# Filling the q and k stacks by 36 transfers inside SBUF instead of a DRAM round trip

## The chip, the cores and the metric

The kernel runs on one core of one Trainium2 chip. The core has five instruction streams that run side by side and meet only at semaphores: PE (TensorE, matrix products), DVE (VectorE), ACT (ScalarE), POOL (GpSimd) and SP (SyncE, which here does nothing but start DMAs). The metric is the device time of one execution in microseconds. Lower is better.

## The reference

The reference is one transformer block. Its first half is a layer norm and a causal linear attention with 16 heads of 16 numbers each; its second half is a layer norm and a mixture of eight experts of which each token uses two.

```python
q = elu(x @ Wq + bq) + 1;  k = elu(x @ Wk + bk) + 1;  v = x @ Wv + bv
s, z = s + outer(k_i, v_i), z + k_i            # over 2048 positions
value_i = (q_i @ s) / (q_i . z + 1e-6)
x = x + values @ Wo + bo
x = x + moe(layernorm(x))                      # top 2 of 8 experts, gelu
```

The input is 4 sequences of 2048 tokens with 256 features, in float32.

## The kernel before

**Stages.** The attention works in 16 steps of 128 positions of all four sequences (512 tokens a step). The recurrence is replaced, within a step, by a masked product of scores and, between steps, by a carried state. The program text is written as a pipeline over steps: body `c` does the front of step `c` (normalise, project q, k and v), the scores and values of step `c-1` and the router of step `c-2`. Every engine has its own copy of `body`, and the order of the work is that of the code on each engine; nothing is scheduled by a planner. Bodies 0 and 1 (the front of the first two steps) are shorter than the others, and body 1 is run in two halves: first its front alone, then its back. After the 16 steps come the tables of the router and then the expert phase, some 71 tiles, which uses none of what is changed.

**Stacks.** PE multiplies in float16. To keep precision, q and k are each split in a high and a low part (`qkhl`, written by ACT at L905 for the high part and by POOL at L1567, or DVE at L1265 in the first two steps, for the low part). A score product has a contraction of only 16 numbers a head, so the kernel stacks three products (high q with high k, low q with high k, high q with low k) for two heads over each other: 96 rows. `kst` and `qst` hold these stacks. Each has two buffers, used in turn by even and odd steps. A row of `qkhl` is a feature on one of 128 partitions, a row of a stack is the same feature on another partition, so the data must cross partitions, and a DMA does that.

**The fill before.** SP writes q's four parts to DRAM (L391, 512 KB), waits for the landing, and reads them back with six loads (L414, 128 KB each). Then it does the same for k, with three loads (L409, 256 KB each). In the first two steps both writes go out first. What frees `qkhl` for the next step is the landing of the write to DRAM (`q_out`, `k_out`, waited for by ACT in `qk_high`). PE waits for all nine loads ahead of the first scores of a step (L559 to L562).

**What else is in SP's queue.** SP runs its DMAs in the order of the code. In a body it is: the load of `xs` for the next step (L375), the store of an output (L378), the load of `xr` (L382), the fill, and then the load of a chunk of the expert weights into `w1raw` (L418 in body 1, L422 otherwise). ACT converts each chunk (`w1_high`, L931). In the second half of body 1 ACT does that between two scores:

```python
                if bk:
                    out_hi(s, 0)
                    score_hi(1, 2)
                    score_hi(1, 3)
                if ro:
                    row_copy(0)
                if c == 1 and not front:
                    w1_high()
```

The landing of the chunk thus stands ahead of ACT's part of the score `(2, 0)` (L875). DVE's `attention_weight` (L1406) gives `wsplit_lo`, which guards the first fill, because the raw weights lie in `kst` at first.

Of the kernel before, what the change touches and what calls it, by code (L numbers as in the profile page):

```python
# [23 lines left out]
P = 128  # L24
B, S, D = 4, 2048, 256
H, HD = 16, 16
E, F = 8, 512
T = B * S
C = 128
# [29 lines left out]
C_TOKEN, C_END = C_PAD + PADS, C_PAD + PADS + STEPS * B  # L59
H_TRI, H_ONES, H_END = 0, 128, 256  # L60
# [27 lines left out]
def build(nc, x, wqkvo, bqk, bv, bo, rw, w1, b1, w2, b2, cf, ch, cb, out):  # L88
    qk_dram = nc.dram_tensor("qk_parts", (2, 2, 4, P, B * C), F16, kind="Internal").ap()
# [4 lines left out]
    with ExitStack() as ctx:  # L94
        def sem(name):
            return ctx.enter_context(nc.semaphore(name))
# [141 lines left out]
        xn_done, xr_in, xr_done = sem("xn_done"), sem("xr_in"), sem("xr_done")  # L238
        xT_ps, xT_hi, xT_lo = sem("xT_ps"), sem("xT_hi"), sem("xT_lo")
        qk_ps, qk_neg, qk_lin, qk_f = sem("qk_ps"), sem("qk_neg"), sem("qk_lin"), sem("qk_f")  # L240
        qk_hi, qk_lo, q_out, k_out = sem("qk_hi"), sem("qk_lo"), sem("q_out"), sem("k_out")
        stack_in = [sem("stack_in0"), sem("stack_in1")]
# [113 lines left out]
        def _(sp):  # L356
# [10 lines left out]
            def body(j, c, front=True, back=True):  # L367
# [3 lines left out]
                lead = fr and c < 2  # L371
# [7 lines left out]
                if fr:  # L379
                    par = c % 2  # L380

                    sp.dma_start(xr[:, par], x_steps[bass.ds(i, 1)].rearrange("i p b d -> p (i b) d")).then_inc(xr_in, 16)  # L382

                    rows = qk_dram[par].rearrange("t (h k) p n -> t h (k p) n", h=2)
                    def send(t, sent):
                        sp.wait_ge(qk_hi, 4 * i + 2 * t + 2)
                        sp.wait_ge(qk_lo, 4 * i + 2 * t + 2)
                        if c >= 2 and t == 0:

                            sp.wait_ge(stack_in[par], 144 * (j + c // 2))  # L390
                        sp.dma_start(qk_dram[par, t].rearrange("m p n -> p m n"), qkhl[:, t]).then_inc(sent, 16)  # L391

                    if lead:
                        send(0, q_out)
                        send(1, k_out)
                    for t, sent in enumerate((q_out, k_out)):
                        if not lead:
                            send(t, sent)
                        sp.wait_ge(sent, 16 * i + 16)
                        if t == 0 and c >= 2:  # L400

                            sp.wait_ge(sc_ps, 16 * (i - 1))
                        elif t == 0:
                            sp.wait_ge(wsplit_lo, 4)
                            sp.wait_ge(qst_zero, 2)
                        for part in range(3):
                            if t == 1:
                                src = rows[1, part // 2].rearrange("(a r) n -> r a n", r=2 * HD)
                                sp.dma_start(kst[2 * HD * part:2 * HD * (part + 1), par], src).then_inc(stack_in[par], 16)  # L409
                                continue  # L410
                            src = rows[0, part % 2].rearrange("(a e d) n -> e d a n", e=2, d=HD)
                            for e in range(2):
                                r0 = 2 * HD * part + HD * e
                                sp.dma_start(qst[r0:r0 + HD, par, :, e], src[e]).then_inc(stack_in[par], 16)  # L414
# [66 lines left out]
        def _(pe):  # L481
# [9 lines left out]
            def body(j, c, front=True, back=True):  # L491
# [67 lines left out]
                def scores(b, n):  # L559
                    g = 16 * s + 4 * b + n  # L560
                    if b == n == 0:
                        pe.wait_ge(stack_in[sp_], 144 * (j + (c - 1) // 2 + 1))  # L562
                    if not fr and b == 0 and n >= 2:

                        pe.wait_ge(v_done, min(2 * (c + 1), 2 * STEPS))
                    elif not (first_s and 4 * b + n < 2):

                        pe.wait_ge(sc_lo, g - 1 if fr or b == 0 else g - 3)
                    o = score_bank(fr, n)
                    nc.tensor.matmul(o[:], ident16, mask16, start=True, stop=False, skip_group_check=True)  # L570
                    for e in range(2):
                        pr = 2 * n + e
                        mm = nc.tensor.matmul(o[:, e * 2 * C:(e + 1) * 2 * C], kst[0:STACK, sp_, pr, b * C:(b + 1) * C],  # L573
                                              qst[0:STACK, sp_, pr, :, b * C:(b + 1) * C], start=False, stop=(e == 1),
                                              skip_group_check=True)
                    mm.then_inc(sc_ps, 1)
# [248 lines left out]
        def _(act):  # L825
# [27 lines left out]
            def body(j, c, front=True, back=True):  # L853
# [47 lines left out]
                def qk_high(m):  # L901
                    act.wait_ge(qk_f, 4 * i + m + 1)
                    if c >= 1:
                        act.wait_ge(q_out if m < 2 else k_out, 16 * i)
                    nc.scalar.activation(qkhl[:, m // 2, m % KC], feature_rows(m, par), ACT.Copy).then_inc(qk_hi, 1)  # L905
# [628 lines left out]
        def _(pool):  # L1534
# [6 lines left out]
            def add_bo(i, c):  # L1541
                pool.wait_ge(xr_in, 16 * i + 16)
                G.tensor_tensor(xr[:, c % 2], xr[:, c % 2], bos[:].unsqueeze(1).to_broadcast([P, B, D]), ALU.add).then_inc(xr_done, 1)
# [177 lines left out]
```

## Time and profile before

| | us |
|---|---|
| median of 3 runs | 1066.47 |
| lowest and highest | 1064.33 and 1066.49 |
| the profiled execution | 1070.12 |
| its span, first to last instruction | 1068.0 |

The profiled execution is 3.65 us above the median of the runs. All moments below are counted from the start of its span. The attention takes about the first 620 us, of which a step in the middle takes about 36.8 us; the expert phase begins at about 650 us.

In the rows, `SPq` is SP's queue of DMA instructions: the time there is that of issuing the DMA and not of moving the data. "To landing" is the time from the start of the issue to the last completion. `[x <-Y]` behind a row is the idle time of the engine ahead of it and what ended it.

### The profile page before, as it was taken

How to read it: one execution, taken by the hardware profiler on the slowest of the kernel's cores; microseconds unless marked ns; L12 is line 12 of the kernel's file. 1: busy time of each engine (PE TensorE's matmuls, PEld its weight loads, DVE VectorE, ACT ScalarE, POOL GpSimd, SP SyncE). 2: the span in 40 equal slices, each digit the busy share in tenths (PEclk: the TensorE clock that was granted, in tenths of full speed). 3: DMA queues.
4: the chain of work that ended last, by engine and by line, in shares of the span. 5: the costliest groups of instructions: out<-in, count | busy, mean ns of one | idle time of the engine just before them, and what ended most of it. 6: DMA issues, size and time to landing. Idle time of an engine off the chain costs nothing.

```text
span 1068.0 us, 31902 instructions
## 1 busy us (share of the span) xinstructions
PE 941.2 (88%) x10010; PEld 771.1 (72%) x10011; DVE 835.4 (78%) x2220; ACT 657.2 (62%) x1248; POOL 670.5 (63%) x580
## 2 busy tenths in 40 slices
PE   6789889988898898899888925899999999999995
PEld 3467667766776676677667723678999999999994
DVE  5779999999999999999998775456666666666663
ACT  8667776777677767767775332445555555555552
POOL 2226587787778777877878452356656656555665
PEclk9899999999999999999999856999999999999998
DMA  5916956546655664566455282355555565555554
GB/s 156 214 58 169 256 145 169 149 138 172 159 123 157 160 174 117 157 170 144 140 154 141 87 313 73 62 81 84 99 93 90 94 98 87 93 98 90 89 98 49
DMA packets 127242, 138.84 MB, mean 130 GB/s; under 512 B 12400, under 2 KB 120304, under 8 KB 126512
## 3 DMA queue, kind: packets, MB, share of 16 engines
q1 hardware_dynamic: 100288, 101.45, 38.1%
q0 software_dynamic: 25680, 35.01, 17.9%
q10 hardware_dynamic: 1184, 1.18, 0.4%
q8 instruction: 56, 0.92, 0.4%
q14 instruction: 34, 0.28, 0.1%
HBM read 71.08 MB, written 66.53 MB: 129 GB/s over the span
## 4 chain that ended last, share of the span: by engine, by line
PE 42%; DVE 35%; issue 8%; DMA 6%; ACT 3%; POOL 3%; SPq 1%; POOLq 0%; DVEq 0%; ACTq 0%
PE pF L488 9%; DVE ahl L1132 8%; PE pS L488 8%; PE pU L488 7%; PE pA L488 4%; DVE xn L1145 4%; PE pO L488 4%; DMA out<-yt,to_token 3%; DVE xn L1233 2%; PE pO L594 2%; DVE pd L1216 2%; DVE st L1111 2%; DVE w1s L1252 2%; ACT ahl L875 2%; DVE v L1192 2%
## 5 line engine op out<-in xcount | busy, mean ns | idle before, releaser
L1680 POOL DMA_INDIRECT out<-yt,to_token x135 | 218.1, 1615 | 178.5 <-DVE yt L1528 90.8
L875 ACT ACTIVATE ahl<-pS 128x512 f16<-128x512 f32 x240 | 141.0, 599 | 82.5 <-PE pS L573 80.9
L1132 DVE SCALAR_TENSOR_TENSOR ahl<-pS,ahl 128x512 f16<-128x512 f32 x240 | 160.8, 680 | 19.8 <-ACT ahl L875 19.4
L1581 POOL DMA_INDIRECT expert_in<-xn,cur x128 | 129.1, 1009 | 35.1 <-issue 33.4
L570 PE MATMUL pS<-cbs 128*128 128x512 bf16 x240 | 92.8, 387 | 23.8 <-DVE ahl L1132 19.9
L1055 ACT ACTIVATE g<-pS,b1s 128x256 f32<-128x256 f32 (+1 forms) x140 | 57.3, 462 | 87.9 <-PE pS L488 87.9
L1494 DVE TENSOR_TENSOR ghl<-g,ghl 128x1024 f16<-128x1024 f32 (+1 forms) x68 | 83.0, 1220 | 20.9 <-ACT ghl L1080 20.9
L488 PE MATMUL pS<-gT,w1s 128*128 128x256 f16 (+1 forms) x840 | 96.4, 271 | 1.0 <-DVE gT L1489 0.9
L488 PE MATMUL pF<-w2s,ghl 128*128 x816 | 95.1, 273 | 2.0 <-issue 1.1
L1539 POOL TENSOR_TENSOR rs<-ve,cfs 128x4 f32<-128x4 f32 x31 | 32.2, 1040 | 102.3 <-DVE ve L1102 102.3
L488 PE MATMUL pF<-xT,was 128*128 128x512 f16 x384 | 93.0, 379 | 3.1 <-DVE xT L1137 2.5
L488 PE MATMUL pU<-w2s,ghl 128*128 x804 | 93.9, 273 | 1.2 <-issue 1.1
L573 PE MATMUL pS<-qst,kst 96*128 96x256 f16 x480 | 93.2, 275 | 0.0
L594 PE MATMUL pO<-vhl,ahl 128*128 128x17 f16 x3072 | 87.5, 171 | 4.9 <-DVE ahl L1132 3.3
L594 PEld LDWEIGHTS pO<-vhl,ahl 128*128 128x128 f16 x3072 | 85.3, 96 | 9.1 <-DVE ahl L1132 8.5
L488 PEld LDWEIGHTS pS<-gT,w1s 128*128 x840 | 80.9, 99 | 11.7 <-issue 2.1
L488 PEld LDWEIGHTS pF<-w2s,ghl 128*128 128x128 f16 x816 | 79.5, 98 | 12.1 <-issue 2.7
L488 PEld LDWEIGHTS pU<-w2s,ghl 128*128 128x128 f16 x804 | 78.3, 98 | 11.3 <-issue 1.9
L1055 ACT ACTIVATE g<-pO,b1s 128x256 f32<-128x256 f32 (+1 forms) x72 | 29.2, 459 | 77.5 <-PE pO L488 77.5
L573 PEld LDWEIGHTS pS<-qst,kst 96*128 96x128 f16 x480 | 47.8, 100 | 34.6 <-issue 1.4
L1080 ACT ACTIVATE ghl<-g 128x1024 f16<-128x1024 f32 (+1 forms) x68 | 72.1, 1060 | 0.1
L488 PE MATMUL pA<-was,aT 128*128 128x256 f16 x384 | 54.8, 280 | 16.5 <-DVE aT L1173 14.9
(193 smaller groups left out, 2293.0 us busy)
## 6 DMA issues: line engine op xcount, KB each, us to landing
xg<-expert_in SPq DMA_DIRECT2D x64, 260.0 KB, 3.1
qk_parts<-qkhl SPq DMA_DIRECT2D x32, 512.0 KB, 2.9
qst<-qk_parts SPq DMA_DIRECT2D x96, 128.0 KB
kst<-qk_parts SPq DMA_DIRECT2D x48, 256.0 KB
xs<-x SPq DMA_DIRECT2D x16, 512.0 KB, 5.4
xr<-x SPq DMA_DIRECT2D x16, 512.0 KB, 4.9
out<-x SPq DMA_DIRECT2D x16, 512.0 KB, 3.2
expert_in<-pads SPq DMA_DIRECT2D x16, 260.0 KB, 3.9
```

The source lines that it names most:

```text
L488: mm = nc.tensor.matmul(out, lhs(a, k), rhs(b_, k), start=(t == 0), stop=(t == len(terms) - 1))
L570: nc.tensor.matmul(o[:], ident16, mask16, start=True, stop=False, skip_group_check=True)
L573: mm = nc.tensor.matmul(o[:, e * 2 * C:(e + 1) * 2 * C], kst[0:STACK, sp_, pr, b * C:(b + 1) * C], qst[0:STACK, sp_, pr, :, b * C:(b + 1) ...
L594: mm = nc.tensor.matmul(pO[:, h * VC:(h + 1) * VC], ahl[:, b % 2, a, h * C:(h + 1) * C], vhl[:, sp_, b_, b, h * VC:(h + 1) * VC], start=False,
L875: nc.scalar.activation(ahl[:, b % 2, 0, n * 4 * C:(n + 1) * 4 * C], score_bank(fr, n)[:], ACT.Relu).then_inc(sc_hi, 1)
L1055: nc.scalar.activation(g[:, p1, f, h * P:h * P + width], hidden[p1][f // 2][:, c0:c0 + width], ACT.Gelu, bias=b1s[:, bass.ds(e * FC + f, 1 ...
L1080: nc.scalar.activation(ghl[:, p1, 0, :, 0:n], g[:, p1, :, 0:n], ACT.Copy).then_inc(g_hi, 1)
L1132: V.scalar_tensor_tensor(ahl[:, b % 2, 1, cols], score_bank(fr, n)[:], 0.0, ahl[:, b % 2, 0, cols], ALU.max, ALU.subtract).then_inc(sc_lo, 1)
L1145: V.scalar_tensor_tensor(xn2[:, rp, b, 0:D], x1[:, b], mv2[:, b, 0:1], rs2[:, b:b + 1].to_broadcast([P, D]), ALU.subtract, ALU.mult).then_ ...
L1494: V.tensor_tensor(ghl[:, p1, 1, :, 0:n], g[:, p1, :, 0:n], ghl[:, p1, 0, :, 0:n], ALU.subtract).then_inc(g_lo, 1)
L1581: G.indirect_dma_start(xg_dram, bass.IndirectOffsetOnAxis(ap=cur[:, qp, 2 * b + t:2 * b + t + 1], axis=0), xn2[:, qp, b], None).then_inc(s ...
L1680: G.indirect_dma_start(out, bass.IndirectOffsetOnAxis(ap=to_token[:, c % 2, s:s + 1], axis=0), yt[:, c % 2, s], None, compute_op=ALU.add). ...
```

## The change

`qkhl` is copied straight into the stacks by DMAs from SBUF to SBUF. An access pattern in SBUF can have only one dimension of partitions, so the block of eight head pairs that one load from DRAM reached is cut in four: a q transfer moves 16 partitions by two pairs (32 KB) and a k transfer 32 partitions by two pairs (64 KB). There are 24 of the first kind and 12 of the second for each step. The DRAM tensor is gone. The order in the queue is: 16 q transfers when the high part of q is there, 8 when the low part is there, 8 k transfers for the high part, 4 for the low part. `qkhl` is free when these transfers have landed, so ACT's `qk_high` now waits for `q_in` and `k_in` of the step before.

```diff
-                    rows = qk_dram[par].rearrange("t (h k) p n -> t h (k p) n", h=2)
-                    def send(t, sent):
-                        sp.wait_ge(qk_hi, 4 * i + 2 * t + 2)
-                        sp.wait_ge(qk_lo, 4 * i + 2 * t + 2)
-                        if c >= 2 and t == 0:
-
-                            sp.wait_ge(stack_in[par], 144 * (j + c // 2))
-                        sp.dma_start(qk_dram[par, t].rearrange("m p n -> p m n"), qkhl[:, t]).then_inc(sent, 16)
...
+                    def q_rows(part):
+                        for e in range(2):
+                            for a in range(PAIRS // KC):
                                 r0 = 2 * HD * part + HD * e
-                                sp.dma_start(qst[r0:r0 + HD, par, :, e], src[e]).then_inc(stack_in[par], 16)
+                                p0 = 2 * HD * a + HD * e
+                                lo = KC * (part % 2)
+                                sp.dma_start(qst[r0:r0 + HD, par, a::PAIRS // KC, e],
+                                             qkhl[p0:p0 + HD, 0, lo:lo + KC]).then_inc(q_in[par], 16)
+
+                    def k_rows(part):
+                        for a in range(PAIRS // KC):
+                            lo = KC * (part // 2)
+                            sp.dma_start(kst[2 * HD * part:2 * HD * (part + 1), par, a::PAIRS // KC],
+                                         qkhl[2 * HD * a:2 * HD * (a + 1), 1, lo:lo + KC]).then_inc(k_in[par], 16)
+
+                    if c >= 2:
+
+                        sp.wait_ge(sc_ps, 16 * (i - 1))
+                    else:
+                        sp.wait_ge(wsplit_lo, 4)
+                        sp.wait_ge(qst_zero, 2)
+                    sp.wait_ge(qk_hi, 4 * i + 2)
+                    q_rows(0)
+                    q_rows(2)
+                    sp.wait_ge(qk_lo, 4 * i + 2)
+                    q_rows(1)
+                    sp.wait_ge(qk_hi, 4 * i + 4)
+                    k_rows(0)
+                    k_rows(1)
+                    sp.wait_ge(qk_lo, 4 * i + 4)
+                    k_rows(2)
...
                     if b == n == 0:
-                        pe.wait_ge(stack_in[sp_], 144 * (j + (c - 1) // 2 + 1))
+                        pe.wait_ge(q_in[sp_], 16 * Q_LOADS * (j + (c - 1) // 2 + 1))
+                        pe.wait_ge(k_in[sp_], 16 * K_LOADS * (j + (c - 1) // 2 + 1))
...
                     if c >= 1:
-                        act.wait_ge(q_out if m < 2 else k_out, 16 * i)
+                        if m < 2:
+                            act.wait_ge(q_in[1 - par], 16 * Q_LOADS * (j + (c - 1) // 2 + 1))
+                        else:
+                            act.wait_ge(k_in[1 - par], 16 * K_LOADS * (j + (c - 1) // 2 + 1))
```

The load of `xr` gets one semaphore for each buffer instead of one for both. No engine's compute instructions change in kind, number or order.

The first place is SP's queue at the start, from the fill of step 0 to the weight chunk. This is the kernel before (`xs`, `xr` are loads of the input, the brackets name the semaphores waited for):

```order
L391 DMA qk_parts<-qkhl 128x4x512 [waits qk_lo,qk_hi] x2
L414 DMA qst<-qk_parts 16x8x512 [waits qst_zero,wsplit_lo,q_out]
L414 DMA qst<-qk_parts 16x8x512 x5
L409 DMA kst<-qk_parts 32x8x512 [waits k_out]
L409 DMA kst<-qk_parts 32x8x512 x2
L375 DMA xs<-x 128x4x256 [waits xn_done]
L382 DMA xr<-x 128x4x256
```

and this the changed kernel at the same place:

```order
L390 DMA qst<-qkhl 16x2x512 [waits qk_hi,qst_zero,wsplit_lo]
L390 DMA qst<-qkhl 16x2x512 x15
L390 DMA qst<-qkhl 16x2x512 [waits qk_lo]
L390 DMA qst<-qkhl 16x2x512 x7
L396 DMA kst<-qkhl 32x2x512 [waits qk_hi]
L396 DMA kst<-qkhl 32x2x512 x7
L396 DMA kst<-qkhl 32x2x512 [waits qk_lo]
L396 DMA kst<-qkhl 32x2x512 x3
L375 DMA xs<-x 128x4x256 [waits xn_done]
L382 DMA xr<-x 128x4x256
```

Between the front of step 0 and the loads of `xs` and `xr` stand 36 DMAs instead of 11. The fill of step 1, which follows, has the same form, and the load of `w1raw` (L418) comes behind it.

The second place is ACT's stream in the front of step 1, where the high parts are written (`et`, `lt` are the pieces of elu). Before:

```order
L905 ACTIVATE qkhl<-qf 128x512 [waits q_out,qk_f]
L889 ACTIVATE et<-pF,negb 128x512 [waits qk_f,qk_ps]
L890 ACTIVATE lt<-pF,linb 128x512
L895 ACTIVATE et<-et,cfs 128x512 [waits qk_neg]
L905 ACTIVATE qkhl<-kf 128x512 [waits k_out,qk_f] x2
```

and in the changed kernel:

```order
L909 ACTIVATE qkhl<-qf 128x512 [waits q_in0,qk_f]
L890 ACTIVATE et<-pF,negb 128x512 [waits qk_f,qk_ps]
L891 ACTIVATE lt<-pF,linb 128x512
L896 ACTIVATE et<-et,cfs 128x512 [waits qk_neg]
L909 ACTIVATE qkhl<-kf 128x512 [waits k_in0,qk_f] x2
```

Nothing has moved there; the semaphores waited for are others. The third place is SP's queue in a later step, from one fill to the next weight chunk, before:

```order
L391 DMA qk_parts<-qkhl 128x4x512 [waits stack_in1,qk_lo,qk_hi]
L414 DMA qst<-qk_parts 16x8x512 [waits sc_ps,q_out]
L414 DMA qst<-qk_parts 16x8x512 x5
L391 DMA qk_parts<-qkhl 128x4x512 [waits qk_lo,qk_hi]
L409 DMA kst<-qk_parts 32x8x512 [waits k_out]
L409 DMA kst<-qk_parts 32x8x512 x2
L422 DMA w1raw<-w 128x512 [waits w1_lo]
```

and in the changed kernel:

```order
L390 DMA qst<-qkhl 16x2x512 [waits qk_hi,sc_ps]
L390 DMA qst<-qkhl 16x2x512 x15
L390 DMA qst<-qkhl 16x2x512 [waits qk_lo]
L390 DMA qst<-qkhl 16x2x512 x7
L396 DMA kst<-qkhl 32x2x512 [waits qk_hi]
L396 DMA kst<-qkhl 32x2x512 x7
L396 DMA kst<-qkhl 32x2x512 [waits qk_lo]
L396 DMA kst<-qkhl 32x2x512 x3
L422 DMA w1raw<-w 128x512 [waits w1_lo]
```

The first transfer no longer waits for the low part of q, and no transfer waits for a landing in DRAM.

## Rows read from the trace of the kernel before

**Rows 1.** The page, part 1: busy time, share, instructions of each engine.

```profile
PE 941.2 (88%) x10010; PEld 771.1 (72%) x10011; DVE 835.4 (78%) x2220; ACT 657.2 (62%) x1248; POOL 670.5 (63%) x580
```

**Rows 2.** Busy time by stretch: length, five engines, granted clock, DMA share, GB/s.

```profile
300.00:400.00 100.00, 90.50 (x1147) 72.02 (x1145) 94.07 (x258) 71.74 (x137) 75.35 (x64) 1.00 0.62 157
```
**Rows 3.** SP's queue in time, middle steps: start, us, line, instruction, count.

```profile
323.39 0.39 SPq L375 DMA_DIRECT2D xs<-x  x1
335.24 0.39 SPq L378 DMA_DIRECT2D out<-x  x1
346.67 2.69 SPq L414 DMA_DIRECT2D qst<-qk_parts  x6
409.00 0.39 SPq L378 DMA_DIRECT2D out<-x  x1
445.81 0.39 SPq L378 DMA_DIRECT2D out<-x  x1
```

**Rows 4.** Waits of PE from 434 to 444: total us, times, longest.

```profile
PE pS L570 <- DMA kst<-qk_parts: 0.5, 1, 0.5
```

**Rows 5.** PE in time, around the first scores of a middle step.

```profile
325.74 0.39 PE L570 MATMUL pS<-cbs 128*128 128x512 bf16 x1
...
327.82 0.44 PE L611 MATMUL pA<-cfs,at 128*128 128x128 f32 x2 [1.47 <-DVE at L1159]
```

**Rows 6.** The chain that ended last, in the same step: start, us, what.

```profile
328.11 1.20 DVE xT L1137 x2
```

**Rows 7.** ACT in time, the same step.

```profile
303.88 0.62 ACT L905 ACTIVATE qkhl<-qf 128x512 f16<-128x512 f32 x1
...
329.80 0.63 ACT L931 ACTIVATE w1s<-w1raw 128x512 f16<-128x512 f32 x1
```

**Rows 8.** The chain that ended last, at the start of the kernel.

```profile
47.75 7.53 DMA w1raw<-w
```

**Rows 9.** All q loads, by tile: issue ns min/median/max, first and last start.

```profile
L414 SPq DMA_DIRECT2D qst<-qk_parts x96: 320/430/2177, 26.0 to 570.8; - x96
```

**Rows 10.** DVE in time, the weight split that guards the first fill.

```profile
21.73 0.68 DVE L1406 SCALAR_TENSOR_TENSOR was<-kst,was 128x512 f16<-128x512 f32 x1
```

**Rows 11.** SP's queue in time, start of the kernel.

```profile
29.47 2.69 SPq L409 DMA_DIRECT2D kst<-qk_parts  x3
32.21 0.45 SPq L375 DMA_DIRECT2D xs<-x  x1
32.70 0.51 SPq L382 DMA_DIRECT2D xr<-x  x1
...
46.29 1.42 SPq L409 DMA_DIRECT2D kst<-qk_parts  x3
```

**Rows 12.** ACT in time, step 1.

```profile
33.97 0.63 ACT L905 ACTIVATE qkhl<-qf 128x512 f16<-128x512 f32 x1 [0.53 <-DVE qf L1261]
...
38.53 0.63 ACT L905 ACTIVATE qkhl<-kf 128x512 f16<-128x512 f32 x1
...
55.30 0.63 ACT L931 ACTIVATE w1s<-w1raw 128x512 f16<-128x512 f32 x1 [1.78 <-DMA w1raw<-w]
```

**Rows 13.** The weight chunks, by tile: landing.

```profile
DMA to landing us min/median/max: 2.7/5.5/7.5
```

**Rows 14.** The page, part 6: DMAs with count, KB each, median us to landing.

```profile
xg<-expert_in SPq DMA_DIRECT2D x7, 130.0 KB, 2.1
```

**Rows 15.** ACT in time, the last fill.

```profile
561.64 0.62 ACT L905 ACTIVATE qkhl<-qf 128x512 f16<-128x512 f32 x1
```

**Rows 16.** PE in time, first scores of the last step.

```profile
583.49 0.39 PE L570 MATMUL pS<-cbs 128*128 128x512 bf16 x1 [1.39 <-DMA kst<-qk_parts]
```

**Rows 17.** DVE in time, at the same moment.

```profile
582.96 0.43 DVE L1168 TENSOR_TENSOR ut<-pU,cbs 128x272 f32<-128x272 f32 x1
...
584.77 0.69 DVE L1132 SCALAR_TENSOR_TENSOR ahl<-pS,ahl 128x512 f16<-128x512 f32 x1 [1.38 <-ACT ahl L875]
```

**Rows 18.** The view of rows 2 for two microseconds of step 1.

```profile
48.00:50.00 2.00, 2.00 (x35) 1.77 (x33) 0.91 (x4) 0.00 (x0) 0.00 (x0) 0.50 1.17 141
```

More of the change, by code:

```diff
@@ L59 @@
 C_TOKEN, C_END = C_PAD + PADS, C_PAD + PADS + STEPS * B
+Q_LOADS, K_LOADS = 24, 12
 H_TRI, H_ONES, H_END = 0, 128, 256
@@ L88, in build @@
 def build(nc, x, wqkvo, bqk, bv, bo, rw, w1, b1, w2, b2, cf, ch, cb, out):
-    qk_dram = nc.dram_tensor("qk_parts", (2, 2, 4, P, B * C), F16, kind="Internal").ap()
     xg_dram = nc.dram_tensor("expert_in", (ROWS, ROW), F32, kind="Internal").ap()
@@ L237, in build @@
         ln2_st, ln2_mv, ln2_ve, ln2_rs = sem("ln2_st"), sem("ln2_mv"), sem("ln2_ve"), sem("ln2_rs")
-        xn_done, xr_in, xr_done = sem("xn_done"), sem("xr_in"), sem("xr_done")
+        xn_done, xr_in, xr_done = sem("xn_done"), [sem("xr_in0"), sem("xr_in1")], sem("xr_done")
         xT_ps, xT_hi, xT_lo = sem("xT_ps"), sem("xT_hi"), sem("xT_lo")
         qk_ps, qk_neg, qk_lin, qk_f = sem("qk_ps"), sem("qk_neg"), sem("qk_lin"), sem("qk_f")
-        qk_hi, qk_lo, q_out, k_out = sem("qk_hi"), sem("qk_lo"), sem("q_out"), sem("k_out")
-        stack_in = [sem("stack_in0"), sem("stack_in1")]
+        qk_hi, qk_lo = sem("qk_hi"), sem("qk_lo")
+        q_in = [sem("q_in0"), sem("q_in1")]
+        k_in = [sem("k_in0"), sem("k_in1")]
         v_ps, v_done, v_hi, v_lo = sem("v_ps"), sem("v_done"), sem("v_hi"), sem("v_lo")
@@ L370, in body @@
                 fr, ro, nx = front and real(j, c), real(j, c - 2), front and real(j, c + 1)
-                lead = fr and c < 2
                 if nx:
@@ L380, in body @@
                     par = c % 2
-                    sp.dma_start(xr[:, par], x_steps[bass.ds(i, 1)].rearrange("i p b d -> p (i b) d")).then_inc(xr_in, 16)
-                    rows = qk_dram[par].rearrange("t (h k) p n -> t h (k p) n", h=2)
-                    def send(t, sent):
-                        sp.wait_ge(qk_hi, 4 * i + 2 * t + 2)
-                        sp.wait_ge(qk_lo, 4 * i + 2 * t + 2)
-                        if c >= 2 and t == 0:
-                            sp.wait_ge(stack_in[par], 144 * (j + c // 2))
-                        sp.dma_start(qk_dram[par, t].rearrange("m p n -> p m n"), qkhl[:, t]).then_inc(sent, 16)
@@ L393, in body @@
[L393 to L412, printed above, removed]
-                                r0 = 2 * HD * part + HD * e
-                                sp.dma_start(qst[r0:r0 + HD, par, :, e], src[e]).then_inc(stack_in[par], 16)
@@ new lines, in body @@
+                    sp.dma_start(xr[:, par], x_steps[bass.ds(i, 1)].rearrange("i p b d -> p (i b) d")).then_inc(xr_in[par], 16)
+                    def q_rows(part):
+                        for e in range(2):
+                            for a in range(PAIRS // KC):
+                                r0 = 2 * HD * part + HD * e
+                                p0 = 2 * HD * a + HD * e
+                                lo = KC * (part % 2)
+                                sp.dma_start(qst[r0:r0 + HD, par, a::PAIRS // KC, e],
+                                             qkhl[p0:p0 + HD, 0, lo:lo + KC]).then_inc(q_in[par], 16)
@@ L1541, in add_bo @@
             def add_bo(i, c):
-                pool.wait_ge(xr_in, 16 * i + 16)
+                pool.wait_ge(xr_in[c % 2], 16 * (c // 2) + 16)
                 G.tensor_tensor(xr[:, c % 2], xr[:, c % 2], bos[:].unsqueeze(1).to_broadcast([P, B, D]), ALU.add).then_inc(xr_done, 1)
```

## The prediction, made before the changed kernel was run

> **What bounds the kernel now.** I read the page's busy shares first, then the chain that ended last, and then SP's queue in time, because SP's queue is all that the change touches. The page says PE 88% and DVE 78% [rows 1], but that is a mean over two phases. In a stretch of the attention DVE is busy 94% and PE 90%, and the DMA engines 62% [rows 2]: the middle steps are held by DVE and PE together, and the DMAs are neither idle nor full. The chain there runs through DVE's long list of operations; the reader is to see that no transfer of q or k stands in it between 300 and 340 us.
>
> Is PE ever late for the stack? In one middle step it waited 0.5 us for k's loads [rows 4]. Yet the two steps ahead of that one last 36.88 us each in the mean (335.24 to 409.00), and the one with the wait 36.81 us (409.00 to 445.81) [rows 3]. The wait costs nothing, because PE starts the first score at 325.74 and its next instruction is held until 327.82 by DVE [rows 5], and DVE itself cannot take that score before it has done `xT`, from 328.11 for 1.20 us, to 329.3 [rows 6]. So a stack that lands about 1.5 us later than PE asks for it is still free, and one that lands earlier gains nothing. The whole middle of the attention should not feel a faster round trip.
>
> At two places the chain does go through the fill's queue. At the start, the load of a weight chunk is issued at 47.75 and lands 7.53 us later, at 55.28 [rows 8]; ACT waits 1.78 us for it [rows 12], so it was ready at 53.5. And at the first scores of the last step, PE waits 1.39 us for k [rows 16].
>
> **Part 1: the price of an issue.** The change turns eleven DMAs a step into 36, all on SP. The bytes fall: 1 MB written and 1.5 MB read become 1.5 MB copied. What counts is how long SP needs for one DMA. Ninety-six q loads took 0.43 us each in the median, and the shortest 0.32 [rows 9]. With the gap between two, six of them take 2.69 us, or 0.45 each [rows 3], and the three k loads at the start 47.75 - 46.29 = 1.46 us, or 0.49 each [rows 8, 11]. A k load has twice the bytes of a q load and costs nearly the same, and the small transfers (a quarter of the bytes) have no row of their own. The bounds are 0.32, the shortest, and 0.49. I take 0.46, close to the bulk of the rows, as bytes hardly matter in them. A fill of 36 is then 16.6 us of SP's time, where the nine loads and two writes took about 5, spread between waits.
>
> One more thing sits in those rows: the three k loads of step 0 took 2.69 us where the same three in step 1 took 1.42 [rows 11], and the longest q load took 2.18 [rows 9]. Single issues are held up by 1 us and more. A fill four times as long meets more of these. I take 1.3 us for the fill of step 0, 0.6 for that of step 1 and 2.0 for one in the middle, where more transfers run. For the landing of the last small transfer I take 2.1 us, from 130 KB loads [rows 14].
>
> **Part 2: the start, where it costs.** The fill of step 0 can begin when the last weight split is done, 21.73 + 0.68 = 22.4 [rows 10]. It is issued by 22.4 + 16.6 + 1.3 = 40.3. Then come `xs` and `xr`, which took 1.0 us together (32.21 to 33.21) [rows 11]: 41.3. They were issued 8 us earlier before. The fill of step 1 follows without a pause, as its high parts are there by then (below): 41.3 + 16.6 + 0.6 = 58.5. Only now can the weight chunk go out. Its landing took 2.7 us at the least and 5.5 in the median, with other loads ahead of it [rows 13]; ahead of it are now only small copies, so I take 2.9: 61.4. Before it was 55.28. That is **+6.1 us**, and it is on the path: behind ACT's conversion of the chunk stands the score `(2, 0)` in ACT's order, then DVE, then PE, and I find no other chain that runs past that point.
>
> The added waits on ACT lie under this. `q_in` for step 0: the 24th issue starts at 22.4 + 23 x 0.46 + 1.3 = 34.3 and lands at 36.4, so ACT's first `qk_high` of step 1, at 33.97 before [rows 12], is 2.4 us later, and all behind it (`et`, `lt`, PE's projections of k, which wait for these). `k_in`: the last issue starts at 39.8 and lands at 41.9, against 38.53 [rows 12]: 3.4 us later. ACT would thus come to the weight chunk at about 53.5 + 3.4 = 56.9, still ahead of 61.4. If the chunk came early, these 3.4 us less the old wait of 1.8 would be what is left. `xr` of step 1, later by 8 us, holds POOL's addition to it, whose result is needed by no one before the next body.
>
> **Part 3: the middle, nothing.** In a middle step the fill starts when the high part of q is written, 303.88 + 0.62 = 304.5 [rows 7]. It is issued by 304.5 + 16.6 + 2.0 = 323.1 and lands by 322.6 + 2.1 = 324.7, a microsecond ahead of PE at 325.74 [rows 5], and PE could bear about 1.5 more. The weight chunk goes out at about 323.1, lands by 328.6 even at the median, and ACT takes it at 329.80 [rows 7]. `xs` had its place at 323.39 [rows 3] and keeps it within a microsecond; it is needed in the middle of the next body. ACT's `qk_high` of the next step comes some 30 us after the fill began. Price: 0, with a cover of 1 to 2.5 us.
>
> **Part 4: the last step, a gain.** The last fill starts at 561.64 + 0.62 = 562.3 [rows 15], is issued by 562.3 + 16.6 + 1.3 = 580.2, and lands by 579.7 + 2.1 = 581.8. PE's wait until 583.49 goes, 1.39 us [rows 16]. DVE is busy until 582.96 + 0.43 = 583.4 and took the score at 584.77 [rows 17], so it can use 1.4 us: **-1.4 us**. What is late next is DVE itself.
>
> **The sum.** Against the profiled execution's own time: 1070.12 + 6.1 - 1.4 = 1074.8. That execution is 3.65 above the median, so on the scale of the runs it is 1066.47 + 4.7 = **1071.2 us**. The expert phase is as before.
>
> **A rule that speaks against this.** The Trainium skill (DMA: Bandwidth & Descriptors, section "Issuing engines are not separate DMA queues") says that the time a sequencer takes to start a DMA is usually small beside the DMA itself. By that, part 2 would vanish and the time would be that of rival 2 below. The rows above do not agree for transfers of this size: 0.43 us to issue whatever the bytes. The same page (section "Rules for kernel authors") asks to coalesce many small transfers and calls those under 64 KB mostly overhead; rival 3 is what that would do if the overhead were larger than the rows show.
>
> **The rivals.** (1) The issue is somewhat cheaper, 0.38 us, since a quarter of the bytes also means a quarter of the rows per DMA. For it speaks the 0.32 minimum [rows 9], against it that k and q loads hardly differ. Each 0.01 us less moves the weight chunk by 0.72 us (72 issues), so this is 5.8 us less, -1.1 in all: 1065.4, no change that can be seen. (2) **Faster.** The small transfers issue at 0.32 us, the shortest of the rows. The chunk would land at 61.4 - 10.1 = 51.3, ahead of ACT; its whole wait of 1.78 goes, and the 1.4 at the end: 1066.47 - 3.2 = 1063.3. This needs at most 0.35 us an issue. Against it: only few of the issues in the rows are that short, and those follow a pause. (3) **Much slower.** An issue in a long burst costs 0.55 us, because the queue backs up. Then the start is +6.1 + 6.5, the fill in the middle lands at 304.5 + 19.8 + 2.0 + 1.6 = 327.9, some 0.6 past what PE can bear, in 12 steps 7 us: about 1084. It decides from about 0.53 on. The longest single issues (2.18 [rows 9]) speak for it, the bulk against it. (4) The clock. PE was granted half its speed, 1.2 instead of 2.4 GHz, at 48 to 50, after it had been idle [rows 18]. A longer idle time ahead of the weight chunk can put such a stretch on the path: about 3 us more, 1074.
>
> **How the numbers follow.** The forecast, 0.42 to 0.50 us an issue, has 0.50 and reaches from 1068.3 to 1074.1, or to 1076 with more held-up issues; rival 1 has 0.20, rival 2 0.12, rival 3 0.10, rival 4 0.08. Less than about 0.2%, 2.1 us, can't be told from no change here. Faster by more than that is rival 2 with the edge of rival 1: 0.13. Within it are the rest of rival 1 and the low edge of the forecast: 0.23. Slower: 0.64. The range of 1064 to 1078 leaves out rival 2's lower half and rival 3.
>
> **What would show it.** In the changed profile: SP's q and k issues at 0.46 us each, 72 of them between 22.4 and 58.5 with a pause of 1 us; the weight chunk (L418) issued near 58 and ACT (L935) idle for it for 4 us or so; a middle step still 36.8 us long and no wait of PE for `kst` that lengthens it; no wait for it at the last step. If the step in the middle changes its length either way, part 3 is wrong; if L418 is issued before 53, the price of an issue is.

## The result and the profile after

The changed kernel takes **1147.44 us** in the median of 4 runs (1146.3 to 1150.87). In the same comparison the kernel before takes 1065.8 (4 runs, 1064.33 to 1066.49). The ratio is 1.0773, with an interval of 1.0746 to 1.0801. The forecast was 1071.2 with a range up to 1078: the sign was right and the size far too small, 4.7 us against 81.6.

The profiled execution has a span of 1148.8 us against 1068.0. First the busy times of the page and one stretch of the attention, in the form of [rows 1] and [rows 2]:

```profile
PE 964.9 (84%) x10010; PEld 788.7 (69%) x10011; DVE 813.1 (71%) x2220; ACT 656.5 (57%) x1248; POOL 669.1 (58%) x580
```

```profile
300.00:400.00 100.00, 86.01 (x1001) 66.69 (x1000) 80.98 (x229) 69.05 (x132) 68.89 (x58) 0.93 0.39 106
213.00:216.00 3.00, 2.56 (x11) 1.83 (x12) 0.88 (x2) 1.10 (x3) 2.82 (x2) 0.50 0.92 279
```

DVE fell from 94% to 81% and the DMA engines from 62% to 39%: the kernel moves less and computes less densely. Neither is the new bound, so the answer must lie in a queue that counts as neither. The chain that ended last gives 7% to SP's issues (`SPq`), where it gave them 1% before:

```profile
PE 59%; DVE 13%; issue 11%; SPq 7%; DMA 5%; POOL 3%; ACT 2%; POOLq 0%; DVEq 0%; ACTq 0%
```

**The price of one issue.** All q and all k transfers by tile: issue in ns as minimum, median and maximum. These lines answer to [rows 9].

```profile
L390 SPq DMA_DIRECT2D qst<-qkhl x384: 585/593/1804, 22.8 to 652.4; - x192
L396 SPq DMA_DIRECT2D kst<-qkhl x192: 586/597/1869, 39.3 to 661.3; - x192
```

The *shortest* of 576 issues takes 0.585 us. With the gap between two it is some 0.64: twelve of them take 7.63 us where none is held up (64.97, below). The load of the weight chunk behind the fill, from DRAM as before, also takes 0.59 (0.58 at 72.64, 0.59 at 211.93), where it took 0.45 before.

**The start.** SP's queue in time; it answers to [rows 8] and [rows 11]:

```profile
22.82 16.45 SPq L390 DMA_DIRECT2D qst<-qkhl  x24
39.31 7.92 SPq L396 DMA_DIRECT2D kst<-qkhl  x12
47.27 0.59 SPq L375 DMA_DIRECT2D xs<-x  x1
47.90 0.54 SPq L382 DMA_DIRECT2D xr<-x  x1
48.55 16.38 SPq L390 DMA_DIRECT2D qst<-qkhl  x24
64.97 7.63 SPq L396 DMA_DIRECT2D kst<-qkhl  x12
72.64 0.58 SPq L418 DMA_DIRECT2D w1raw<-w  x1
```

SP issues without a pause for 50 us. The chain at this place is the list of these issues one by one, and ends in the landing of the chunk, at 72.64 + 3.09 = 75.73 instead of 55.28:

```profile
72.64 3.09 DMA w1raw<-w
```

What waited, between 20 and 80 us (total us, times, longest), where [rows 12] had one wait of 1.78:

```profile
POOL xr L1547 <- DMA xr<-x: 20.3, 1, 20.3
ACT w1s L935 <- DMA w1raw<-w: 16.3, 1, 16.3
...
ACT qkhl L909 <- DMA qst<-qkhl: 7.0, 1, 7.0
...
ACT qkhl L909 <- DMA kst<-qkhl: 3.4, 1, 3.4
```

The first two are the longest. Only ACT's is on the path: the chain goes from the landing of the chunk to ACT's score behind it. How far this shifts the program is read from the sixteen stores of output, whose first and last starts are, in the kernel before and in the changed one:

```profile
L378 SPq DMA_DIRECT2D out<-x x16: 377/389/782, 77.8 to 618.5; - x16
```

```profile
L378 SPq DMA_DIRECT2D out<-x x16: 383/384/799, 98.2 to 699.5; - x16
```

The first store is 20.4 us late, as late as the chunk landed (75.73 - 55.28 = 20.45). The last one is 81.0 us late. So 20.4 us arose at the start, 60.6 in the fifteen intervals between, and nothing behind: the span is longer by 80.8.

**A middle step.** SP's queue, in the form of [rows 3]:

```profile
180.17 0.38 SPq L378 DMA_DIRECT2D out<-x  x1
...
186.79 16.33 SPq L390 DMA_DIRECT2D qst<-qkhl  x24
203.16 8.72 SPq L396 DMA_DIRECT2D kst<-qkhl  x12
211.93 0.59 SPq L422 DMA_DIRECT2D w1raw<-w  x1
...
221.35 0.38 SPq L378 DMA_DIRECT2D out<-x  x1
```

From one store to the next it is 41.18 us, where a middle step of before took 36.8 [rows 3]. PE at the first score, against [rows 5]:

```profile
206.92 1.04 PE L518 MATMUL pF<-cfs,xn 128*128 128x128 f32 x8
213.44 0.58 PE L571 MATMUL pS<-cbs 128*128 128x512 bf16 x1 [5.49 <-issue]
213.82 0.63 PE L574 MATMUL pS<-qst,kst 96*128 96x256 f16 x2
```

The view says "issue" and not "DMA kst": it finds no completion to put the wait down to, so the cause has to be read from SP's rows. The issue of the last k transfer begins at 211.3, and 2.1 us later, at 213.4, PE goes on. And PE does not go on at full speed: the granted clock is 0.50 from 213 to 216 (the row of that stretch is above), so that a pair of score products takes 0.63 us instead of 0.38. The same is seen behind the next three of these waits (0.50 from 254 to 257, 295 to 298 and 336 to 339). Over 110 to 540 us PE's waits before the score begin with:

```profile
ACT ahl L876 <- PE pS L574: 93.3, 82, 5.9
DVE ahl L1136 <- ACT ahl L876: 66.7, 60, 3.6
...
PE pS L571 <- issue: 51.9, 10, 5.6
```

Ten waits of 5.2 us each. The delay is passed on to ACT and DVE: their two waits were 52.2 and 9.9 us in the same window before.

The sixteen stores of output give fifteen intervals. The third to the thirteenth last 40.95 us in the mean (40.28 to 41.71), 4.13 longer than the 36.82 of before: 45.4 us in all. The first two together are 8.6 longer (45.01 + 36.98 against 37.18 + 36.23), so 4.3 each; they are uneven because the store between them stands in SP's queue behind sixteen writes of constants, which themselves stand behind the fill. The fourteenth, with the last fill, is 6.9 longer (38.78 against 31.90), the fifteenth 0.3 shorter.

### The profile page after: what moved, and what is told of

The parts are those of the page before. It is cut to its first block, busy times and chain, and to the rows that moved or that the text cites. A ratio compares the mean times of both kernels' runs of the same rounds, so it can differ in the third digit from the quotient of the medians.

```text
span 1148.8 us, 32271 instructions
## 1 busy us (share of the span) xinstructions
PE 964.9 (84%) x10010; PEld 788.7 (69%) x10011; DVE 813.1 (71%) x2220; ACT 656.5 (57%) x1248; POOL 669.1 (58%) x580
## 4 chain that ended last, share of the span: by engine, by line
PE 59%; DVE 13%; issue 11%; SPq 7%; DMA 5%; POOL 3%; ACT 2%; POOLq 0%; DVEq 0%; ACTq 0%
PE pF L488 13%; PE pS L488 7%; PE pU L488 6%; PE pA L488 6%; PE pO L595 5%; PE pS L571 4%; SPq L390 4%; PE pS L574 4%; PE pO L488 3%; DVE xn L1149 3%; DMA out<-yt,to_token 3%; DVE ahl L1136 3%; PE pU L604 2%; SPq L396 2%; DVE st L1115 2%
## 5 line engine op out<-in xcount | busy, mean ns | idle before, releaser
L571 PE MATMUL pS<-cbs 128*128 128x512 bf16 x240 | 99.1, 413 | 78.9 <-issue 73.2
L488 PE MATMUL pF<-xT,was 128*128 128x512 f16 x384 | 99.0, 397 | 3.2 <-DVE xT L1141 2.7
L574 PE MATMUL pS<-qst,kst 96*128 96x256 f16 x480 | 100.2, 292 | 0.0
L571 PEld LDWEIGHTS pS<-cbs 128*128 128x128 bf16 x240 | 24.5, 102 | 93.5 <-issue 78.4
L488 PEld LDWEIGHTS pU<-w2s,ghl 128*128 128x128 f16 x804 | 78.3, 98 | 11.0 <-issue 1.7
```

Source lines behind the costliest of these rows:

```text
L488: mm = nc.tensor.matmul(out, lhs(a, k), rhs(b_, k), start=(t == 0), stop=(t == len(terms) - 1))
```

## The experiments

The experiments ran on two chips, on which the kernel before has 1074.4 (chip 12) and 1075.48 (chip 11) instead of 1065.8, so times are compared by the ratio to it. Of the changed kernel itself there is no run on these two chips; so where its ratio and that of a version differ by a point or so, the chip is not ruled out as the reason.

### forms: what makes an issue dear

The kernel before with 54 extra DMAs at its very end, in nine groups of six; each group has landed before the next is issued. They move data that nothing reads between a weight tile, a scratch tile and DRAM.

```diff
+            for n in range(N):
+                sp.dma_start(zr[16 * n:16 * n + 16, 0:8:4], wr[0:16, 0:2]).then_inc(form_in[0], 16)
+            land(0)
...
+            for n in range(N):
+                sp.dma_start(zr[16 * n:16 * n + 16, 0:16:2], dr[0:8, 0:16].rearrange("m p n -> p m n")).then_inc(form_in[4], 16)
+            land(4)
```

> The kernel before, with nine groups of six DMAs put behind its last expert tile, when the DMA queues are nearly idle; its result is not touched, only its end is later. It measures what one DMA costs SP to issue, by form. Theory A (the unequal or strided pattern is dear): SBUF to SBUF with one run of 1024 read and two runs of 512 written costs 0.59 us, and SBUF to SBUF with equal runs on both sides costs 0.43. Theory B (any copy from SBUF to SBUF is dear): all forms with both ends in SBUF cost 0.59, whatever the runs, and the forms with an end in DRAM 0.43. Theory C (a long burst is dear, not the form): every group of six costs 0.43 here.

Issue by group (w2s and w2raw lie in SBUF, qk_parts in DRAM):

```profile
L493 SPq DMA_DIRECT2D w2raw<-w2s x6: 586/595/777, 1058.5 to 1061.9; - x6
L496 SPq DMA_DIRECT2D w2raw<-w2s x6: 516/581/592, 1064.2 to 1067.6; - x6
L499 SPq DMA_DIRECT2D w2raw<-w2s x6: 592/592/632, 1069.6 to 1072.9; - x6
L502 SPq DMA_DIRECT2D w2raw<-w2s x6: 585/1084/1529, 1074.9 to 1080.0; - x6
L505 SPq DMA_DIRECT2D w2raw<-qk_parts x6: 343/430/432, 1085.4 to 1087.6; - x6
L508 SPq DMA_DIRECT2D w2raw<-qk_parts x6: 303/423/425, 1093.1 to 1095.3; - x6
L511 SPq DMA_DIRECT2D w2raw<-w2s x6: 546/601/602, 1097.1 to 1100.3; - x6
L514 SPq DMA_DIRECT2D qk_parts<-w2s x6: 322/420/420, 1102.4 to 1104.6; - x6
L517 SPq DMA_DIRECT2D w2raw<-qk_parts x6: 302/420/422, 1106.1 to 1108.3; - x6
```

L493 has the form of a q transfer (16 partitions, two pieces of 1 KB, 32 KB). L496 is contiguous on both sides, L499 strided on both, L511 one row on each of 128 partitions: 0.58 to 0.60 for all. L508 has the form of L493 but reads DRAM: 0.42. L505 is the old q load: 0.43, as in [rows 9]. L514 writes to DRAM: 0.42. Theory B holds and A and C do not: it is not the pattern, not the direction, not the burst and, L502 aside, not the size (L511 moves four times the bytes of L493). **With both ends in SBUF an issue costs 0.17 us more** than in the same form with one end in DRAM (L493 against L508), on an otherwise quiet queue. Why it does, no run shows. Of the groups only L502, 128 KB between 16 partitions, is dearer still, and there from the third on: the queue backs up.

### contig: the same in place

The stacks laid out so that each transfer writes one contiguous piece a partition.

```diff
-                                sp.dma_start(qst[r0:r0 + HD, par, a::PAIRS // KC, e],
+                                sp.dma_start(qst[r0:r0 + HD, par, e, KC * a:KC * a + KC],
...
-                            sp.dma_start(kst[2 * HD * part:2 * HD * (part + 1), par, a::PAIRS // KC],
+                            sp.dma_start(kst[2 * HD * part:2 * HD * (part + 1), par, KC * a:KC * a + KC],
```

> The changed kernel with the stacks laid out so that each of the 36 transfers reads and writes one contiguous run of 1024 numbers a partition (pairs stored in another order, which the scores follow); same number, same bytes, same waits. Theory A (strided pattern): an issue costs 0.43 to 0.46 us, a middle step 36.8 us, the weight chunk of body 1 issued near 58, about 1071 us in all. Theory B (both ends in SBUF) and theory C (burst): still 0.59 us, a middle step 41.2, about 1147 us.

1145.31 us, ratio 1.0632 (1.0598 to 1.0666). The issue stays:

```profile
L390 SPq DMA_DIRECT2D qst<-qkhl x384: 507/589/1887, 22.5 to 643.9; - x192
```

The layout of the destination is not the cause of the price. The time came out lower than expected, though: the ratio is 1.4 points below that of the change, PE's waits for the first score in the same window are 28.2 us instead of 51.9, and the steps swing between 38.7 and 42.5 us, 40.43 in the mean. The layout need not be what did this: after_chunk (below) has the old layout and shows the same, 26.9 us of waits and steps of 38.8 to 42.2. What makes the steps swing is open.

### two_thirds: fewer transfers, same price

From step 2 on the second copies of the high parts are left out: 24 transfers a step instead of 36. The start is untouched.

```diff
                     q_rows(0)
-                    q_rows(2)
+                    if c < 2:
+                        q_rows(2)
...
                     k_rows(0)
-                    k_rows(1)
+                    if c < 2:
+                        k_rows(1)
```

> The changed kernel with the second copy of the high parts (8 q and 4 k transfers) left out from step 2 on, so 24 transfers instead of 36; the scores then use stale rows there. Theory (SP's time to issue is what makes PE late): the fill takes 24 x 0.636 = 15.3 us and lands some 6 us ahead of PE, the middle step falls from 41.2 to 36.8 us, and the total by about 14 x 4.4 = 60 us, to 1087; the 20 us at the start stay. Rival (the added waits of ACT on the landings, or slow copies, hold the step): it stays above 39 us, and the total above 1115.

1096.81 us, ratio 1.0204 (1.0174 to 1.0235). Its middle step in SP's queue:

```profile
213.62 11.23 SPq L390 DMA_DIRECT2D qst<-qkhl  x16
224.90 5.07 SPq L396 DMA_DIRECT2D kst<-qkhl  x8
230.02 0.58 SPq L424 DMA_DIRECT2D w1raw<-w  x1
```

A fill of 16.3 us, close to the 16.6 that the forecast had assumed for 36. The steps of the middle are 36.80 to 37.01 again, but for two of 38.89 and 37.35. The theory holds, in the total too: 1.0204 x 1065.8 is 1087.5. ACT's added waits on the landings are still there, so they are not what lengthens the step. The first store stays late, at 96.8. This separates the two parts: with a fill of 16 us the middle is nearly free, as part 3 said, and most of what is left is the start. Against the first trace the first store is 19.0 us late and the last 25.0; of the 6.0 between them 2.1 are the one long step and 2.5 the last interval (32.92 against 30.42), which is open.

### before_chunk and after_chunk: the start alone

The weight chunk's load is taken out from behind the fill of step 1: in the kernel before it goes ahead of the reading back, in the changed kernel ahead of the fill.

```diff
                         send(0, q_out)
                         send(1, k_out)
+                        if c == 1:
+                            sp.wait_ge(w1_lo, 1)
+                            sp.dma_start(w1raw[:], w1[:, F:2 * F]).then_inc(w1_in, 16)
...
-                if c == 1 and front:
-
-                    sp.wait_ge(w1_lo, 1)
-                    sp.dma_start(w1raw[:], w1[:, F:2 * F]).then_inc(w1_in, 16)
```

And in the changed kernel:

```diff
+                    if c == 1:
+                        sp.wait_ge(w1_lo, 1)
+                        sp.dma_start(w1raw[:], w1[:, F:2 * F]).then_inc(w1_in, 16)
                     sp.wait_ge(qk_hi, 4 * i + 2)
                     q_rows(0)
```

> The kernel before with one DMA moved: in body 1 the weight chunk is issued ahead of the nine loads of the fill instead of behind them. Theory (ACT's wait of 1.8 us for the chunk is on the path): the chunk lands before ACT asks, 1.8 us faster. Rival (the loads, delayed by it, or the next wait take its place): within 1 us of the kernel before.

> The changed kernel with the weight chunk of body 1 issued ahead of that step's 36 transfers instead of behind them. Theory (in the start the 36 issues of 0.636 us hold the chunk, and with it ACT, which waited 16.3 us): that wait goes, the output of step 0 is stored at 98 - 14 = 84 instead of 98, and the total falls by about 12 to 16 us, to 1131 to 1135; the middle step stays at 41. Rival (the stack of step 1 or the added waits of ACT on the landings hold the start just as long): under 6 us faster.

The changed kernel with the early chunk takes 1136.9 us, ratio 1.0616 (1.0569 to 1.0663). The first store comes at 86.0 instead of 98.2, where 84 was expected. So 12.2 of the 20.4 us were the chunk's place behind 36 issues, and 8.2 stay, in which ACT still waits for the stacks of step 0:

```profile
ACT qkhl L908 <- DMA qst<-qkhl: 6.6, 1, 6.6
ACT qkhl L908 <- DMA kst<-qkhl: 3.1, 1, 3.1
```

Against the kernel before with the early chunk, whose first store comes at 72.6, these stacks cost 13.4 us. The whole fell by 1.57 points of the ratio, 16.7 us, just above the 12 to 16 expected: the steps are also shorter than in the first trace of the change, 40.30 us in the mean. They swing as in contig.

The kernel before with the early chunk takes **1067.31 us, ratio 0.9929 (0.9909 to 0.9949)**: 0.7% faster than the kernel before, clear of the interval, and the best version found. I had expected about 1.8 us, the wait of [rows 12]; it is 7.1 below the 1074.4 on its chip. Its first store comes at 72.6 instead of 77.8.

Why 1.8 was too little is seen in the trace of forms, whose attention is that of the kernel before, on the same chip. In the first trace ACT came late to the chunk, so that its wait was short. A small copy on DVE ran beside POOL's addition to `xr` (42.29 to 44.75) and ended with it, and from 45 to 55 us PE was granted 0.66:

```profile
42.46 2.32 DVE L1296 COPY dummy_token<-cfs 128x16 f32<-128x16 f32 x1
```

```profile
45.00:55.00 10.00, 8.73 (x89) 6.59 (x90) 7.31 (x15) 2.66 (x5) 0.76 (x1) 0.66 1.09 176
```

In forms neither happens. The copy comes before POOL's addition, PE is granted 1.00, and ACT waits 7.14 us for the chunk:

```profile
42.28 0.17 DVE L1337 COPY dummy_token<-cfs 128x16 f32<-128x16 f32 x1
```

```profile
45.00:55.00 10.00, 7.62 (x131) 6.01 (x131) 4.73 (x11) 1.96 (x4) 0.76 (x1) 1.00 1.10 181
```

```profile
56.53 0.63 ACT L972 ACTIVATE w1s<-w1raw 128x512 f16<-128x512 f32 x1 [7.14 <-DMA w1raw<-w]
```

And yet its first store comes at 78.3, as late as in the first trace. So in both it is the chunk that sets the time, and the delays of DVE and PE are hidden under the wait for it. With the early chunk ACT converts it at 50.36 instead of 55.30, without a wait, which is the 5.2 us at the first store. The last store comes 4.6 us earlier than in forms (614.4 against 619.0); the rest of the 7.1 has no place in a trace.

### k_on_act: a second queue for a third of the issues

The twelve k transfers go to ACT's queue, the 24 for q stay with SP.

```diff
+                def k_rows(part):
+                    for a in range(PAIRS // KC):
+                        lo = KC * (part // 2)
+                        act.dma_start(kst[2 * HD * part:2 * HD * (part + 1), par, a::PAIRS // KC],
+                                     qkhl[2 * HD * a:2 * HD * (a + 1), 1, lo:lo + KC]).then_inc(k_in[par], 16)
...
                 if fr:
                     qk_high(3)
+                    if c < 2:
+                        act.wait_ge(wsplit_lo, 4)
+                    else:
+                        act.wait_ge(sc_ps, 16 * (i - 1))
+                    act.wait_ge(qk_hi, 4 * i + 4)
+                    k_rows(0)
+                    k_rows(1)
```

> The changed kernel with the 12 k transfers of a step issued by ACT, in two lots behind its conversion of k, so that two queues issue side by side. Theory (the price is SP's own issue time): SP's fill shrinks to 24 x 0.636 = 15.3 us, PE no longer waits for the stack, but ACT is busy 12 x 0.6 = 7.6 us a step more, 34 of 36.8, and holds the scores: a middle step 38 to 40 us, total 1100 to 1130. Rival (descriptors from SBUF to SBUF are made in one place for both queues): an issue costs well over 0.6 us where the two lots overlap, and the step stays at 41 or more.

1166.7 us (2 runs), ratio 1.0855 (1.0827 to 1.0884): slower than the change itself by 0.8 points, and far above the 1100 to 1130 expected. The rival's step of 41 us or more came, but not for its reason: the price is nearly the same on either queue with both in use (medians of 0.593 us on SP's and 0.618 on ACT's), and SP is done with q in time (15.93 us from 222.38 in one step). At the start it even helps: the first store comes at 89.1 instead of 98.2. The step is 42.4 us in the mean, as now ACT's own work stands still:

```profile
L903 ACTq DMA_DIRECT2D kst<-qkhl x192: 592/618/2087, 24.8 to 662.1; - x192
```

```profile
227.81 5.73 ACTq L903 DMA_DIRECT2D kst<-qkhl  x8
...
236.10 2.55 ACTq L903 DMA_DIRECT2D kst<-qkhl  x4
```

```profile
ACT ahl L865 <- issue: 81.3, 20, 6.6
DVE ahl L1141 <- ACT ahl L865: 63.5, 42, 3.4
```

In the step shown the two lots keep ACT from its scores for 8.3 us (5.73 + 2.55), and over 110 to 540 us ACT stands idle ahead of its scores for 81.3 us that the view puts down to "issue"; DVE then waits for ACT. An issue costs the engine that makes it; it has to go where there is slack ahead of a deadline, and ACT had less than SP.

### k_direct: the round trip kept for q

The kernel before with the early chunk, in which from step 2 on only k goes straight, in twelve transfers behind q's six loads.

```diff
+                        if not lead and t == 1:
+                            for part in range(3):
+                                sp.wait_ge(qk_hi if part < 2 else qk_lo, 4 * i + 4)
+                                for a in range(PAIRS // KC):
+                                    lo = KC * (part // 2)
+                                    sp.dma_start(kst[2 * HD * part:2 * HD * (part + 1), par, a::PAIRS // KC],
+                                                 qkhl[2 * HD * a:2 * HD * (a + 1), 1, lo:lo + KC]).then_inc(stack_in[par], 16)
+                            continue
```

> The kernel before with the early weight chunk, and from step 2 on k alone by the 12 transfers inside SBUF (7.6 us of issue in place of a write, a landing and three loads); q by DRAM as before. Theory (a fill that is issued early enough costs nothing in the middle and only PE's wait of 1.4 us at the last step is to be had): a middle step 36.8 us, total 1.4 us under the kernel before with the early chunk, 6 to 9 us under the kernel before. Rival (a dear issue costs by itself, wherever it stands): 10 us slower than that.

1072.93 us (12 runs), ratio 1.0003 (0.998 to 1.0026): no difference from the kernel before, where the early chunk alone has 0.9929. (By the medians it is 2.55 us below the kernel before; the ratio goes by all runs, of which three took 1079 to 1083.) The expected gain is not there, and the total is nearer to the rival's 10 us. The rival's reason is not seen, however. The middle is untouched (36.8), as the queue has room for 12:

```profile
341.48 2.69 SPq L425 DMA_DIRECT2D qst<-qk_parts  x6
344.22 8.79 SPq L405 DMA_DIRECT2D kst<-qkhl  x12
353.06 0.59 SPq L429 DMA_DIRECT2D w1raw<-w  x1
```

PE's wait of [rows 16] is gone. Yet the last two intervals between stores are 32.92 and 33.03 us, against 31.90 and 30.42 in the kernel before and 31.89 and 31.20 in that kernel with the early chunk. PE was granted 0.91 from 570 to 590 us, where both of these had 1.00. Against the kernel with the early chunk the first store is 0.3 us earlier (72.3) and the last 2.8 later (617.2). From the last store to the end of the span it takes 453.2 us, 3.7 more than in the kernel before; but the five other full-length traces from these two chips (all but forms, which has a longer end) have 451.0 to 452.2 there, so at least 1.5 of that is not this version's. So the wait of part 4 goes and the time does not. What took the 2.9 us of the last two intervals is not settled; the lower clock stands beside it, and this was not tried apart.

## Why the prediction was wrong

**Part 1, the price of an issue: the step that failed.** The forecast put it at 0.46 us within bounds of 0.32 and 0.49. Measured are 0.593 for the issue and some 0.64 with the gap. The bounds were taken from 96 q loads and a few k loads, and *every one of them had one end in DRAM*. They agreed with each other, whatever the bytes, and that was read as "an issue costs this much". It showed only that bytes hardly matter between those two; the property that the change altered, both ends in SBUF, was varied by no row. forms shows that it is this property, and contig that it is not the layout; why the chip takes longer for such an issue stays open. The other term taken from loads with an end in DRAM, the 2.1 us to the landing, came out right (211.3 to 213.4); the rows gave no more reason for that. The hold-ups on top were sized well: a fill of step 0 took 24.45 us, 36 x 0.636 = 22.9 and 1.5 more (forecast 1.3), one in the middle 25.09, so 2.2 more (forecast 2.0).

**Part 2, the start.** The mechanism was right, the size followed from part 1. The chunk was to go out at 58.5 and went out at 72.64: 7.0 us were lost by the end of the fill of step 0 (47.27 against 40.3), 7.2 more by that of step 1. Its landing took 3.1 (2.9 forecast). The program moved by exactly that, 20.4 instead of 6.1. "ACT would come to the weight chunk at 56.9, still ahead of it": it was ready at 59.5 (58.39 + 1.09, its last instruction ahead). The reading that the chunk is what is waited for, and the stacks lie under it, holds: after_chunk removes the one and finds the other, 8.2 us where the forecast had 3.4 less 1.8. What the forecast missed here is that the wait of 1.78 us is not what the chunk cost the kernel before: before_chunk gains 5.2 us at the first store.

**Part 3, the middle: not free.** Three quarters of the loss, 60.6 of 81 us, arose here and in the last step, where the forecast had nothing and a gain. The cover of "1 to 2.5 us" was sized well and the load on it was not. By the forecast's own sum with the measured price: 304.5 + 22.9 + 2.0 - 0.6 + 2.1 = 330.9, against 325.74 + 1.5 = 327.3 that PE could bear: 3.6 us a step. It was 4.13; the slower clock behind the waits is the likely rest, not tried apart. two_thirds, with a fill of the forecast's length, gives the forecast's step. The cover was thinner than the error of the term it covered: over 36 issues, 0.03 to 0.07 us each use it up, which rival 3 says and the range did not take in.

**Part 4, the last step.** Not a gain of 1.4 but a loss of 6.9 in that interval. It is the middle's mechanism: PE waits 6.46 us ahead of the first score of the last step (at 663.44), where it waited 1.39. In k_direct the wait does go, and even there no gain is seen.

**The rivals.** Rival 3 was the one, and dearer still: it was to decide from 0.53, was sized at 0.55 and 1084, and had a chance of 0.10. Its reason was wrong, though: the queue does not back up, since the shortest issue costs as much as the median. By 0.636 in its own sum it would have given 1066.5 + 6.1 + 72 x 0.176 + 12 x 3.6 = 1128, and with the last fill (+6.9) 1135; the other 12 us are one more such step, 0.53 us more in each of the 13, and 1.6 at the start. Rivals 1 and 2 looked for a cheaper issue, rival 1 because the transfers are small; in forms 16 KB and 128 KB from DRAM cost the same (L517 and L505). Rival 4 is there as a follower: a clock at 0.50 behind each of the four waits of 5 us and more that were looked at.

**The rule that speaks against it.** The Trainium skill (DMA: Bandwidth & Descriptors, section "Issuing engines are not separate DMA queues") calls the time to start a DMA usually small beside the transfer. This case's trace does not bear that out for the kernel's time: one copy lands about 2 us after its issue began, but 36 issues occupy SP for 25 of 41 us, and PE waits for the last of them.

## What to carry to other kernels

A DMA costs its issuing engine time whatever it moves; count them, multiply by the price *of that kind* (here 0.59 us with both ends in SBUF, 0.42 with one in DRAM), and set the product against the deadline of the last, not against the bytes saved. Where a bound is taken from the rows of a trace, ask whether any of them varies the property that the change varies; if not, the spread of the rows is no bound. Look at what stands behind a burst in the same queue: a load with a consumer on the path belongs ahead of it, which was worth 0.7% in the kernel before. And do not take the length of a wait in one trace for its price: for the same chunk, ACT waited 1.78 us in one execution and 7.14 in another, with the same first store, since in the first one ACT itself was late.

## What the runs showed of the hardware

- A DMA from SBUF to SBUF was issued in 0.58 to 0.60 us on SP's queue (forms, medians of L493, L496, L499 and L511, with 16 or 128 partitions), and in 0.42 to 0.43 with one end in DRAM (L505, L508, L514, L517). On ACT's queue the first kind took 0.62 in the median (k_on_act). Other DMAs with an end in DRAM lay on both sides of 0.42: in the kernel before 0.39 for the stores of output and 0.51 for the loads of `xr`.
- What stands next behind a burst of SBUF copies was dear too: the load of the weight chunk, from DRAM, took 0.58 to 0.59 there and 0.45 in the kernel before.
- Six copies of 128 KB from 16 to 16 partitions in a row backed the queue up: the issues went from 0.59 to 1.53 us (forms, L502). The same bytes from DRAM did not (L505).
- A single small copy on DVE took 2.32 us when it began beside a POOL addition of 2.46 us and ended with it (the kernel before), and 0.17 us when that addition had not begun (forms, before_chunk).
- Behind waits of PE of 5.0 to 5.6 us the granted clock was 0.50, the level of 1.2 GHz, in the 3 us looked at (the changed kernel, from 213, 254, 295 and 336 us).
